# Graph attention with a gated residual and layer norm: broadcasts and means ahead of the sixth product, prologue reordered, quotients on ScalarE

## What is computed

```python
h = einsum('bnd,ade->bane', feat_in, W)
th = tanh(h)
attn = einsum(th, w_src) + swapaxes(einsum(th, w_dst), 2, 3)
attn = where(attn >= 0, attn, 0.2 * attn)
attn = softmax(where(~adj, -999.0, attn), axis=-1)
feat_out = einsum('banm,bame->bane', attn, h) + b
feat_out = elu(feat_out, heads side by side)
gate = sigmoid(feat_in @ H_w.T + H_b)
return layernorm(feat_in + gate * feat_out + (1.0 - gate) * feat_in)
```

## Time and profile before

| | us |
|---|---|
| median of 3 runs (lowest, highest) | 798.93 (798.83, 800.71) |
| profiled execution, device time | 799.27 |
| its span in the trace | 797.5 |
| PE busy | 724.3 (91%) |
| DVE busy | 711.0 (89%) |
| POOL busy | 536.8 (67%) |
| ACT busy | 374.9 (47%) |

### The profile page before, as it was taken

The page is one execution under the profiler, slowest core; times in us unless marked ns, Lnnn a source line. Parts: engine busy times, 40 slices in busy tenths (PEclk is TensorE's granted clock), DMA queues, the critical chain, the costliest instruction groups (busy, mean ns, idle before and its releaser), DMA issues.

```text
span 797.5 us, 12614 instructions
## 1 busy us (share of the span) xinstructions
PE 724.3 (91%) x3472; PEld 401.5 (50%) x3472; DVE 711.0 (89%) x1277; ACT 374.9 (47%) x804; POOL 536.8 (67%) x380
## 2 busy tenths in 40 slices
PE   4299999999999999999999999999999999999970
PEld 4164564646456464645646454564545455553430
DVE  6668899989989998998999899898989999899885
ACT  4123426355553636555363645536264563626352
POOL 7964386775949677693957769395876939584500
PEclk9599999999999999999999999999999999999995
DMA  5020021112112111211211121211202121110202
GB/s 172 0 94 1 2 91 40 54 41 93 41 50 81 39 53 39 92 39 58 73 39 53 39 92 39 72 59 39 56 36 92 39 85 47 40 24 30 79 1 79
DMA packets 32875, 43.82 MB, mean 55 GB/s; under 512 B 1234, under 2 KB 26580, under 8 KB 32852
## 3 DMA queue, kind: packets, MB, share of 16 engines
q1 hardware_dynamic: 24660, 31.35, 12.5%
q10 hardware_dynamic: 8192, 12.19, 4.2%
HBM read 30.95 MB, written 12.58 MB: 55 GB/s over the span
## 4 chain that ended last, share of the span: by engine, by line
PE 89%; ACT 3%; DVE 3%; issue 2%; POOL 2%; DMA 1%; ACTq 0%; POOLq 0%; DVEq 0%; SPq 0%
PE out_T L798 47%; PE hg L726 27%; PE vb L782 7%; PE tr L806 6%; ACT att_T L400 1%; POOL th_w L257 1%; PE hg L767 1%; PE hg L772 1%; DMA ew<-in_W 1%; DVE ew L592 1%; DVE ex L684 0%; DMA out<-y 0%; PE hg L753 0%; ACT y L433 0%; DVE w_lo L510 0%
## 5 line engine op out<-in xcount | busy, mean ns | idle before, releaser
L592 DVE SCALAR_TENSOR_TENSOR ew<-vb,u,adj_in 128x512 f32<-128x512 f32 x768 | 536.1, 742 | 22.7 <-PE vb L782 22.7
L798 PE MATMUL out_T<-ew,vals 128*64 128x512 f32 x1536 | 392.3, 603 | 1.3 <-DVE ew L592 1.3
L257 POOL TENSOR_TENSOR th_w<-th,score_w 128x768 f32<-128x768 f32 x64 | 134.6, 2105 | 184.0 <-ACT th L371 147.9
L798 PEld LDWEIGHTS out_T<-ew,vals 128*64 128x64 f32 x1536 | 114.0, 136 | 200.6 <-issue 136.2
L400 ACT ACTIVATE att_T<-out_T,tiny 128x512 f32<-128x512 f32 x96 | 66.1, 689 | 245.7 <-PE out_T L798 245.7
L726 PE MATMUL hg<-w_hi,xT_hi 128*128 128x384 f32 x384 | 150.9, 393 | 14.4 <-DVE xT_lo L515 10.4
L726 PE MATMUL hg<-w_lo,xT_hi 128*128 128x384 f32 x384 | 130.2, 339 | 0.0
L726 PE MATMUL hg<-w_hi,xT_lo 128*128 128x384 f32 x384 | 88.5, 338 | 0.0
L726 PEld LDWEIGHTS hg<-w_hi,xT_hi 128*128 128x128 f32 x384 | 74.0, 193 | 25.2 <-issue 23.7
L806 PE MATMUL tr<-ident,att_T 128*128 128x128 f32 x384 | 59.1, 277 | 21.6 <-ACT att_T L400 21.6
L782 PE MATMUL vb<-v_T,head_sel 128*128 128x512 bf16 x192 | 74.4, 390 | 0.7 <-ACT v_T L392 0.7
(11 more groups left out here) (94 smaller groups left out, 718.8 us busy)
## 6 DMA issues: line engine op xcount, KB each, us to landing
xT_in<-in_xT SPq DMA_DIRECT2D x16, 768.0 KB, 4.6
x_in<-in_x SPq DMA_DIRECT2D x16, 768.0 KB, 4.5
out<-y ACTq DMA_DIRECT2D x15, 768.0 KB, 3.5
adj_in<-in_adjT SPq DMA_DIRECT2D x16, 256.0 KB, 4.8
ew<-in_W SPq DMA_DIRECT2D x1, 576.0 KB, 4.2
ew<-in_HwT SPq DMA_DIRECT2D x1, 576.0 KB, 8.0
score_w<-in_w_rows SPq DMA_DIRECT2D x1, 384.0 KB, 6.8
out<-y SPq DMA_DIRECT2D x1, 384.0 KB, 2.5
```

Of the source, the lines that this page charges most:

```text
L257: g.tensor_tensor(th_w[:, c % 2], th[:, c].unsqueeze(1).broadcast_to([P, 2, D]), score_w[:], ALU.mult).then_inc(S["thw_done"], 1)
L592: ve.scalar_tensor_tensor(out=ew[:, (2 * C * j + i) % SLOTS, :], in0=VB[h % 4][:], scalar=u[:, q, c, h:h + 1], in1=adj_in[:, q, c, :], op0 ...
L798: te.matmul(OUT[VW * k:VW * k + VW, :], vals[:, q, c, h, :], ew[:, t % SLOTS, :], start=(c == 0), stop=(c == C - 1)).then_inc(S["ew_free"], 1)
```

## The change

It has these parts:

- **PE:** the first two broadcasts of batch b + 1 leave the inside of product 5 and stand ahead of it, after `transpose_out(b, 4)`. `means(b)` moves from the next step to ahead of `transpose_out(b, 4)` and writes bank `HG[1]`.
- **Banks:** features 0, 1, 2 go to `HG[0]` and 3 to `HG[1]`; gate 0 to `HG[0]` and 1 to 3 to `HG[1]`; the waits follow.
- **ACT and DVE:** the quotients are now made by ACT, eight copies of 128x32 for each product, each with the inverse as a per-partition scale, reading `TR` and writing `att`. They wait for DVE's inverses. They stand after features 1 (product 5 of the batch before), ahead of `copy_out(1)`, (2), (3) and (4), and ahead of `copy_out(5)`. `copy_vT` moves behind `copy_out(4)`. `rden` gets two buffers; everything that counted `att_done` now counts eight per product.
- **ACT features:** tanh first, then the plain copy.
- **Prologue:** DVE clears half of `vals` early and POOL the other half; DVE weighs batch 0's chunks, each right before its head sums; POOL adds the bias, splits the next x, makes the values and only then the sums for the means, for which ACT now waits in the features of batch 1. PE begins its first features with the high products, and waits for the low parts within them.
- **products:** the nine matmuls go in the order high-high, high-low, low-high, each three together.

```diff
-    SETUP = 18
+    SETUP = 19
+    DVE_SETUP = 12
-        rden = sb("rden", [P, C, 2])
+        rden = sb("rden", [P, 2, C, 2])
-        G_BANK = [HG[1], HG[0], HG[1], HG[1]]
+        G_BANK = [HG[0], HG[1], HG[1], HG[1]]
-        mean_ps = HG[0][:, 0:D]
+        mean_ps = HG[1][:, 0:D]
+        QN = 2 * C
-            return HG[0] if c == 3 else HG[1]
+            return HG[1] if c == 3 else HG[0]
...
@@ POOL before() @@
+                g.memset(vals[:, 1], 0.0).then_inc(S["pool_setup"], 1)
                 pool.wait_ge(S["pool_setup"], SETUP)
-                pool.wait_ge(S["ld_cols"], 16)
-                for c in range(C):
-                    weigh(0, c)
-                add_bias(0, 0)
+                add_bias(0)
+                for c in range(C):
+                    split_low(1, 1, c)
+                pool.wait_ge(S["dve_setup"], DVE_SETUP)
                 values(0, 0)
-                for c in range(C):
-                    split_low(1, 1, c)
+                add_rows(0, 0)
...
@@ ACT features(b, c) @@
-                a.activation(h_sb[:, c], feature_bank(b, c)[:, 0:D], ACT.Copy).then_inc(S["hcopy_done"], 1)
+                if isinstance(b, int) and b == 1:
+                    act.wait_ge(S["hb_sum_done"], 1)
                 if not isinstance(b, int) or b:
                     act.wait_ge(S["thw_done"], C * (b - 1) + c + 1)
                 a.activation(th[:, c], feature_bank(b, c)[:, 0:D], ACT.Tanh).then_inc(S["th_done"], 1)
+                a.activation(h_sb[:, c], feature_bank(b, c)[:, 0:D], ACT.Copy).then_inc(S["hcopy_done"], 1)
...
+            def quotients(b, q, j):
+                act.wait_ge(S["inv_done"], HP * b + j + 1)
+                if j == 0 and (not isinstance(b, int) or b > 1):
+                    act.wait_ge(S["elu_done"], b - 1)
+                for c in range(C):
+                    for k in range(2):
+                        h = 2 * j + k
+                        a.activation(att[:, q, c, E * h:E * h + E], TR[:, c * P + VW * k:c * P + VW * k + E], ACT.Copy,
+                                     scale=rden[:, j % 2, c, k:k + 1]).then_inc(S["att_done"], 1)
...
@@ ACT step() @@
                 if not last:
                     features(b + 1, 1)
+                if not first:
+                    quotients(b - 1, 1 - q, HP - 1)
                 copy_out(b, 0)
...
+                quotients(b, q, 0)
                 copy_out(b, 1)
                 gates(b, 0)
                 gates(b, 1)
+                quotients(b, q, 1)
                 copy_out(b, 2)
                 gates(b, 2)
+                quotients(b, q, 2)
                 copy_out(b, 3)
...
                     for c in range(C):
                         split(b + 2, q, c)
+                quotients(b, q, 3)
+                copy_out(b, 4)
                 if not last:
                     copy_vT(b + 1, 1 - q)
-                copy_out(b, 4)
                 if not first:
                     row_squares(b - 1)
+                quotients(b, q, 4)
                 copy_out(b, 5)
...
@@ ACT after() @@
                 gate_quarter(B - 1)
+                quotients(B - 1, (B - 1) % 2, HP - 1)
                 x_forms(B - 1)
...
@@ DVE before() @@
+                ve.memset(vals[:, 0], 0.0).then_inc(S["dve_setup"], 1)
                 dve.wait_ge(S["ld_w"], 16)
...
-                ve.memset(vals[:], 0.0).then_inc(S["dve_setup"], 1)
...
-                for c in range(C):
+                dve.wait_ge(S["ld_cols"], 16)
+                for c in range(C):
+                    dve.wait_ge(S["th_done"], c + 1)
+                    ve.tensor_tensor(th_w[:, c % 2], th[:, c].unsqueeze(1).broadcast_to([P, 2, D]), score_w[:],
+                                     ALU.mult).then_inc(S["thw_done"], 1)
                     head_sums(0, c)
...
@@ DVE attended() @@
-                    ve.reciprocal(rden[:], t[:, :, :, E]).then_inc(S["inv_done"], 1)
-
-                def quotients():
-                    dve.wait_ge(S["inv_done"], HP * b + j + 1)
-                    o = att[:, q].rearrange("p c (h e) -> p c h e", e=E)[:, :, 2 * j:2 * j + 2, :]
-                    ve.tensor_tensor(o, t[:, :, :, 0:E], rden[:].unsqueeze(3).broadcast_to([P, C, 2, E]),
-                                     ALU.mult).then_inc(S["att_done"], 1)
-
-                return [inverses, quotients]
+                    if j > 1 or not isinstance(b, int) or b:
+                        dve.wait_ge(S["att_done"], QN * (HP * b + j - 1))
+                    ve.reciprocal(rden[:, j % 2], t[:, :, :, E]).then_inc(S["inv_done"], 1)
+
+                return [inverses]
 
             def add_means(b, q):
 
-                dve.wait_ge(S["att_done"], HP * b + HP)
+                dve.wait_ge(S["att_done"], QN * (HP * b + HP))
...
@@ PE before() and features of batch 0 @@
-                pe.wait_ge(S["w_lo_done"], 1)
+                pe.wait_ge(S["w_hi_done"], 1)
...
+                    products(feature_bank(b, c), q, c, 0, [],
+                             {KD: (S["w_lo_done"], 1), 2 * KD: (S["xlo_done"], c + 1)}).then_inc(S["h_done"], 1)
...
@@ PE features, later batches @@
-                elif c == 0:
-                    pe.wait_ge(S["gate_done"], C * (b - 1))
+                if c == 0:
+                    pe.wait_ge(S["vT_done"], b)
                 elif c == 3:
-                    pe.wait_ge(S["vT_done"], b)
                     pe.wait_ge(S["att1_done"], C * (b - 1))
                 else:
-                    pe.wait_ge(S["th_done"], C * b + c)
+                    pe.wait_ge(S["hcopy_done"], C * b + c)
...
@@ PE attend() @@
-                        if j == HP - 1 and (c, k) in ((1, 1), (3, 0)) and not last:
-                            broadcast_v(b + 1, 1 - q, c // 2)
...
@@ PE step() @@
                 broadcast_v(b, q, 3)
-                if not first:
-                    pe.wait_ge(S["vT_done"], b + 1)
-                    means(b - 1, 1 - q)
...
                 if not last:
                     transpose_v(b + 1)
+                means(b, q)
                 transpose_out(b, 4)
-                attend(b, q, 5, last)
+                if not last:
+                    broadcast_v(b + 1, 1 - q, 0)
+                    broadcast_v(b + 1, 1 - q, 1)
+                attend(b, q, 5)
 
             def after():
                 transpose_out(B - 1, HP - 1)
-                means(B - 1, (B - 1) % 2)
```

More of the change, by code:

```diff
@@ L277, in values @@
             def values(b, q):
+                pool.wait_ge(S["hb_done"], b + 1)
                 pool.wait_ge(S["exps_done"], NEX * b + 1)
@@ L321, in step @@
                 if not last:
-                    add_bias(b + 1, 1 - q)
+                    add_bias(b + 1)
+                    add_rows(b + 1, 1 - q)
                     values(b + 1, 1 - q)
@@ L713, in before, with products @@
                 broadcast_v(0, 0, 1)
-            def products(bank, q, c, col, extra):
+            def products(bank, q, c, col, extra, waits={}):
                 o = bank[:, 0:D]
@@ L720, in products @@
                 for k in range(KD):
-                    mms += [(xT_hi[:, q, k, n], w_hi[:, k, col:col + D]), (xT_hi[:, q, k, n], w_lo[:, k, col:col + D])]
+                    mms.append((xT_hi[:, q, k, n], w_hi[:, k, col:col + D]))
+                for k in range(KD):
+                    mms.append((xT_hi[:, q, k, n], w_lo[:, k, col:col + D]))
                 for k in range(KD):
@@ L725, in products @@
                 for i, (l, r) in enumerate(mms):
+                    if i in waits:
+                        pe.wait_ge(*waits[i])
                     last = te.matmul(o, l, r, start=(i == 0), stop=(i == len(mms) - 1))
@@ L729, in features @@
             def features(b, q, c):
+                if isinstance(b, int) and b == 0:
+                    pe.wait_ge(S["xhi_done"], c + 1)
+                    if c > 1:
+                        pe.wait_ge(S["hcopy_done"], c - 1)
+                    products(feature_bank(b, c), q, c, 0, [],
+                             {KD: (S["w_lo_done"], 1), 2 * KD: (S["xlo_done"], c + 1)}).then_inc(S["h_done"], 1)
+                    return
                 pe.wait_ge(S["xhi_done"], C * b + c + 1)
                 pe.wait_ge(S["xlo_done"], C * b + c + 1)
[L733 to L737 removed]
+                if c == 0:
+                    pe.wait_ge(S["vT_done"], b)
                 elif c == 3:
[L739 removed]
                     pe.wait_ge(S["att1_done"], C * (b - 1))
                 else:
[L742 removed]
+                    pe.wait_ge(S["hcopy_done"], C * b + c)
                 products(feature_bank(b, c), q, c, 0, []).then_inc(S["h_done"], 1)
@@ L746, in max_T @@
                 pe.wait_ge(S["scores"], NSC * b + 1)
-                if not isinstance(b, int) or b:
-                    pe.wait_ge(S["gate_done"], C * (b - 1) + 2)
+                if isinstance(b, int) and b == 0:
+                    pe.wait_ge(S["hcopy_done"], C)
+                else:
+                    pe.wait_ge(S["gate_done"], C * (b - 1) + 1)
```

(22 more changed lines are left out.)

21 lines of the change are left out of this document (10 added, 11 removed).

## The result

Before 798.90 (798.83 to 800.71, four runs), after **814.96** (814.89 to 816.1, four runs): ratio 1.0199 [1.0181, 1.0216], slower by 16.1 where 13.7 were forecast. The profiled execution of after took 815.02, its span is 813.2, 15.7 more than before's 797.5.

The account below looks back on a forecast made before the run. PE and DVE both nearly full, ACT half empty (period 46.28). Prologue -7.6, batch 0 -1.9, batch 1 +.6, twelve periods +18, batch 14 +.4, last +2.8 and +1.4: +13.7, median 812.6; forecast's own range 803 to 822.

Parts of the forecast that it names:

- Part 1: Broadcasts ahead of the sixth product on PE: pairs stay whole, 1.2 less per batch, DVE's 1.30 wait goes.
- Part 2: Means (.83) moved to PE's gap after the fifth product, banks swapped, tanh before copy on ACT: gains nothing.
- Part 3: Quotients from DVE to ACT: DVE saves 2.0 per batch, ACT gains 48 copies of 316 ns, .21 apart.
- (a): Fourth group of quotients on ACT, ahead of product 5's copy: sixth product ends 13.4 after the fourth, before 14.4.
- (b): Last product's quotients, queued on ACT behind normalisation and features 1: done 8.8 after the sixth product, DVE's add_means 4.0 late.
- What DVE makes up: DVE from add_means to the fifth product's end: 33.8 falls to 31.95 through four quotients (1.36) and a wait (.51).
- Part 4: Prologue: DVE weighs and shares the clearing with POOL; first attention product at 36.5 instead of 44.33, gain 7.6 (5.5 to 9).
- The edges: Batches outside the twelve full periods: batch 0 -1.9, batch 1 +.6, batch 14 +.4, the last +2.8 and +1.4.
- (1): Rival: small copies on ACT are cheap, .13 apart; period 46.5, 795, faster; chance .11.
- (2): Rival: PE decides alone, DVE's sixteen score slots absorbing the last product's late quotients; 771; chance .09.
- (3): Rival: ACT's copies don't overlap; 49.5 per period, 836; chance .06.
- (4): Rival: in between, copies .17 apart, or prologue better by 3 and seam milder by .8; about no change; chance .08.

Follow-up runs that it names:

- e6: The changed kernel with the two broadcasts put back inside the sixth product: 838.41 us, ratio 1.0476.
- e7: The kernel before with nothing but the two broadcasts moved ahead of the sixth product: 780.37 us, ratio .9752.
- e1: The changed kernel with all six groups of quotients back on DVE, everything else of the change kept: 764.99 us, ratio .9571.
- e3: The changed kernel with the last product's quotients moved on ACT from behind features 1 to ahead of the normalisation: 760.8 us, ratio .9516.
- d2: The changed kernel with the last product's quotients made twice, the spare copies first (8 more copies per batch): 840.51 us, ratio 1.0492.
- d1: The changed kernel with the quotients of the first three products each made twice (24 more small copies per batch): 827.49 us, ratio 1.0357.
- d4: The changed kernel with the quotients of the first two products made twice (16 more small copies per batch): 827.20 us, median of three runs, ratio 1.0331.
- d3: The changed kernel with two extra 128x704 copies on ACT ahead of the quotients of each of the first three products: 817.31 us, ratio 1.0215.

## Why the prediction held, and where it was off

The mechanism held: group 6 behind the normalisation on ACT makes the loss. That the sum came within 2.0 of the time is in part luck, since its errors cancelled. Copies closer together than forecast made each period .64 shorter, a longer way of DVE made it .86 longer, and the edges were wrong by 3.5 and by -4.1. With the measured spacing of .175 alone, the forecast's own two sums (.21 apart gives 813, .13 apart gives 795) would have given about 805 by interpolation. The points in turn:

- **Part 1 (1.2 on PE a batch, DVE's wait of 1.30 gone): right.** The product with its two broadcasts takes 409.47 - 405.35 = 4.12 (forecast 4.1, before 5.37). On the path it is worth 1.36 and 1.37 (e6, e7).
- **Part 2 (nothing): held for the means, not for the order of ACT's copies.** The means run from 403.03 in the gap after A5, and PE still waits .97 for the copy behind them. PE still waits for the second features copy too, .59 here. But e1 has 44.39 where e7 has 44.91. The traces place the .52: from the end of the fifth product to the end of the sixth e7 takes 399.25 - 392.94 = 6.31 and e1 386.63 - 380.81 = 5.82, while from there to the end of the first product both take the same (8.56 and 8.55), with the means in it and without. In e1 ACT makes `copy_out(4)` ahead of `copy_vT`, so the wait of e7 before the transposes is gone (timelines of PE, e7 and then e1). In after group 4 stands in that place and eats the gain. No run moved the copies alone.

```profile
394.60 0.66 PE L804 MATMUL tr<-ident,att_T 128*128 128x128 f32 x4 [1.27 <-ACT att_T L400]
```

```profile
381.74 0.64 PE L853 MATMUL tr<-ident,att_T 128*128 128x128 f32 x4
```

- **Part 3, price of a copy (316 ns, .21 apart; bounds .13 to .32): duration right, spacing too wide.** 312 ns, but eight take 1.54, (1.54 - .31) / 7 = .175 apart. The scale operand does cost (a bare 128x48 takes 232); the overlap is .137, not the .1 read from the wide copies of line 433. The .175 lies below the .19 to .23 that the forecast's own range was worked out with. The Trainium skill ("ScalarE: Activation LUTs", rules for kernel authors) was weighed in the prediction: read as a price on the path it gave 130. The trace does not bear that out: e3, with all 48 copies, is 4.2 faster than e1, with none (1.0 of it lies ahead of the first mark, .15 a batch is in the periods).
- **(a) Sixth product 13.4 after the fourth: 409.47 - 396.41 = 13.06**, by the spacing. Before 14.38, so 1.3 gained.
- **(b) Group 6: started 6.98 after A6 (forecast 7.0), `add_means` 8.55 after A6 (forecast 8.85), DVE idle 3.86 (forecast about 4.25).** The core of the argument, and e3 and d2 show that it is the cause: moved away the loss is gone, doubled it grows by just its own length.
- **What DVE makes up (31.95 from `add_means` to the next A5): too short, 32.81.** Of the .86 some .6 is the elu, 2.35 where 1.76 was forecast. DVE's delay let POOL's weighing start first, and the two exclude each other (below); that step took 1.76 from the earlier trace rows without asking who runs beside it. The other .3 are two waits of DVE that grew: .56 for PE's transposes where before had .36, and .85 for ACT's `hg` (line 396) where before had .77.
- **Period:** 47.8 - .34 (spacing, in a) - .30 (in b) + .86 = 48.02, measured 48.04 in the trace's middle and 47.995 in the mean. Twelve of them cost 20.6, not 18: 2.6 more.
- **Part 4 (-7.6, first score 30.0, first product 36.5): -7.61 at the mark, 30.38 and 36.71.** Start of after, all engines, and the earlier trace rows before it:

```profile
14.64 0.96 DVE L557 TENSOR_TENSOR th_w<-th,score_w 128x768 f32<-128x768 f32 x1
...
20.21 3.20 DVE L557 TENSOR_TENSOR th_w<-th,score_w 128x768 f32<-128x768 f32 x1
...
24.43 0.23 DVE L575 TENSOR_REDUCE d_max_c<-sd 128x12 f32<-128x48 f32 x1
...
30.38 6.68 DVE L622 SCALAR_TENSOR_TENSOR ew<-vb,u,adj_in 128x512 f32<-128x512 f32 x10 [2.25 <-PE vb L818]
...
36.71 3.65 PE L832 MATMUL out_T<-ew,vals 128*64 128x512 f32 x16
```

- **The edges: their sum right by luck (+3.3 forecast, +2.7 by the marks), their parts wrong both ways.** The first two batches: forecast -1.9 + .6, measured +2.19 (+.25 and +1.94: the second is already a full period of 48.03). Without the normalisation in front, group 6 of batch 0 still starts 5.8 after A6 (80.31 against 74.49), since the copies of features 1 ahead of it now wait 2.01 for PE's own products; that wait I had not named, and `add_means` is 2.6 late. The last two: forecast .4 + 2.8 + 1.4, measured -.42 + .95. In the last seam `add_means` is 2.6 late too (6.72 after A6, before 4.11), but A6 itself comes 3.0 earlier after its mark (29.76, before 32.80), a gain that the +2.8 left out; the 1.4 for the last group stands (1.97 from inverses to x + 1, before .62). So of the 15.7 - 13.7 = 2.0 that the sum lacked, 2.6 are the twelve periods, 3.5 the first two, and -4.1 the last.
- **The rivals.** (1) Copies .13 apart: excluded by .175 and by the period. (2) PE decides, 771: its stated condition, group 6 done 4.84 after A6, was not met in after; e3 meets it (done 4.48 after) and is at 760.8, 10 better than the rival's price. That PE alone decides there is not shown: PE is busy 42.68 of 44.25. (3) No overlap: excluded by 1.54 for eight. (4) In between, .17 apart, about no change: its spacing came true (.175) and its time did not. Its price was too low for that spacing (805 by the interpolation above), and DVE's longer way added the rest.

## What to carry to other kernels

Before moving work to a half-empty engine, write down for each moved group what stands ahead of it in that engine's queue and which in-order engine waits for it: here four of six groups cost nothing (1 to 3 could be doubled without a longer period until the step in ACT's loop; behind group 5 the copy still waits .59 for PE in after's trace), one cost .75 a batch, and the sixth turned a gain of 40 (e3, against its own run of before) into a loss of 16. If a change has several parts, price them one by one, as here they added: prologue 7.3, broadcasts 1.37 a batch, and the one misplaced wait hid both. The cure here was to move one call, not to give the work back.

## What the runs showed of the hardware

**DVE and POOL exclude each other on such pairs, and who starts first decides who pays.** Before, the elu (419.26, 1.76) started first, and POOL's weighing behind it took 2.64 in place of 1.82; after, POOL is first and the elu pays. POOL in the two kernels, timelines of before and of after:

```profile
420.06 2.64 POOL L257 TENSOR_TENSOR th_w<-th,score_w 128x768 f32<-128x768 f32 x1 [2.82 <-ACT th L371]
```

```profile
422.54 1.82 POOL L259 TENSOR_TENSOR th_w<-th,score_w 128x768 f32<-128x768 f32 x1 [4.46 <-DVE sd L570]
```

The elu of after took 2.31 in the mean of fifteen, 1.76 before. In e3 the elu is first again (395.03, 1.76), and POOL's weighing (395.45) took 3.03. In the prologue of after one of DVE's weighings took 3.20 beside POOL's bias work, the others .96. The Trainium skill ("SBUF — State Buffer", section "SBUF: two separate sides") has a rule for it: a DVE instruction with two SBUF inputs and a POOL one that reads SBUF share one pair of ports, and the first holds it for its whole length. By that rule, the trace agrees in both orders.

**ACT's loop has a step in its cost.** Between 16 and 32 instructions added to a loop of 198 timed ones, each return of the loop begins to cost 2.0 to 2.2 (d1, d4 against d2, d3). That it goes by the count, or what grows with it, and not by ACT's time is shown by d3; what in the chip it is, is not.

**The time at which PE's clock rises differs between kernels that are alike up to there.** After and e6, windows at the start (window, then length, busy PE, PEld, DVE, ACT, POOL, granted clock):

```profile
38.00:41.00 3.00, 3.00 (x16) 1.25 (x13) 1.89 (x3) 0.56 (x1) 1.22 (x1) 1.00 0.00 0
```

```profile
38.00:41.00 3.00, 3.00 (x12) 1.71 (x12) 3.00 (x5) 0.87 (x2) 0.76 (x1) 0.64 0.00 0
```

After is at 1.00 (2.4 GHz) there, e6 still partly at the lower level (1.2 GHz), and its first mark comes at 45.86 where after has 42.74. Of e6's 23.4 over after this explains 3.1, of d2's 25.6 (mark 45.90) 3.2. Before and e7, the same code up to there, have their first marks at 50.35 and 52.30. What decides it stays open, and it need not be the kernel: the runs of one kernel spread about as much (e6 835.88 to 838.67), though only one of each has a trace. So a difference of up to 3 between two kernels here is to be read from the periods, not from the times.
